# Six PSUM banks divided anew between two kinds of attention scores: from three and three to four and two

## The reference

```
x = x + attention(layernorm(x))          # 32 heads of 16, 8 key/value heads, so groups of 4 query heads
x = x + ffn(layernorm(x))                # silu(x Wg') * (x Wu') Wd', inner width 1376
attention: q, k rotated by position (rotary); att = q k' / 4, causal mask, softmax, times v, times Wo
```

## Time and profile before

| | us |
|---|---|
| median of 3 runs | 824.01 |
| lowest, highest | 822.51, 1285.82 |
| profiled execution, its own time | 827.75 |
| span of its profile, first to last instruction | 826.0 |
| granted TensorE clock, mean of the span | 0.978 |

### The profile page before, as it was taken

One profiled execution on the slowest core, in us unless ns is written; L12 is line 12 of the kernel. 1 busy time (PEld: TensorE's weight loads), 2 busy tenths in 40 slices (PEclk: granted clock), 3 DMA queues, 4 the chain that ended last, 5 costly groups with the idle time before them and its releaser, 6 DMA issues.

```text
span 826.0 us, 12351 instructions
## 1 busy us (share of the span) xinstructions
PE 778.1 (94%) x4449; PEld 529.0 (64%) x4480; DVE 437.5 (53%) x744; ACT 345.0 (42%) x684; POOL 208.0 (25%) x380
## 2 busy tenths in 40 slices
PE   3879999999999999999797999999999999999998
PEld 2645555555555554444385887888878888788886
DVE  6786878677876777887243543423314233241112
ACT  3326667766776677656542332211112111121111
POOL 3134774467526763233300000000000000000000
PEclk9959999999999999999998999999999999999999
DMA  7235677233232335471195110422003210020001
GB/s 254 72 102 175 218 247 230 80 97 111 74 112 73 108 97 185 130 206 36 41 291 151 51 39 13 141 64 66 25 14 130 73 55 34 13 102 0 1 1 51
DMA packets 74614, 81.86 MB, mean 99 GB/s; under 512 B 8721, under 2 KB 58385, under 8 KB 74353
## 3 DMA queue, kind: packets, MB, share of 16 engines
q1 hardware_dynamic: 74560, 81.16, 31.7%
HBM read 57.02 MB, written 33.36 MB: 109 GB/s over the span
## 4 chain that ended last, share of the span: by engine, by line
PE 46%; SPq 2%; DMA 1%; DVE 1%; issue 0%; ACT 0%; DVEq 0%
PE bank L1458 31%; PE ps_y L1510 14%; SPq L1277 1%; SPq L1274 1%; PE bank L1497 1%; DMA inverse<-scratch_inverse 0%; DMA wd_lo<-scratch_wd_raw 0%; DVE x_in L1440 0%; SPq L172 0%; SPq L173 0%; DVE x_res L1444 0%; DVE o_in L185 0%; DVE ctx_lo L195 0%; DVE wd_lo L1384 0%; ACT wd_hi L1332 0%
## 5 line engine op out<-in xcount | busy, mean ns | idle before, releaser
L846 DVE TENSOR_REDUCE m_raw<-ps_s 128x1 f32<-128x512 f32 (+3 forms) x352 | 210.8, 634 | 63.1 <-PE ps_s L1091 60.9
L716 ACT ACTIVATE probs<-ps_t 128x512 f32<-128x512 f32 (+1 forms) x352 | 185.8, 564 | 101.8 <-PE ps_t L1118 100.5
L1415 DVE TENSOR_TENSOR h<-h,bank 128x512 f32<-128x512 f32 (+1 forms) x44 | 30.2, 687 | 221.2 <-PE bank L1458 220.3
L1088 PE MATMUL ps_s<-k_rows,q_rows 96*128 96x256 bf16 (+3 forms) x512 | 132.6, 312 | 6.8 <-DVE m_raw L846 6.1
L1118 PE MATMUL ps_t<-q_rows,k_rows 98*128 98x512 bf16 (+1 forms) x352 | 126.3, 363 | 3.1 <-ACT probs L716 0.9
L1353 ACT ACTIVATE h<-bank 128x512 f32<-128x512 f32 (+1 forms) x44 | 26.3, 599 | 153.4 <-PE bank L1458 153.4
L1088 PEld LDWEIGHTS ps_s<-k_rows,q_rows 96*128 96x128 bf16 x512 | 44.4, 100 | 70.4 <-DVE m_raw L846 32.4
L1131 PE MATMUL ps_o<-probs,v_ones 128*32 128x512 f32 (+3 forms) x1024 | 84.3, 447 | 0.6 <-ACT o_sb L726 0.4
L624 POOL TENSOR_SCALAR_AFFINE_SELECT probs<-probs 128x512 f32<-128x512 f32 x128 | 84.6, 661 | 0.0
L1359 ACT CAST h_hi<-h 128x512 fp32r<-128x512 f32 (+1 forms) x44 | 27.4, 622 | 126.9 <-DVE h L1415 126.9
L217 POOL TENSOR_TENSOR var_eps<-mean_var,eps 128x1 f32<-128x1 f32 x16 | 3.0, 189 | 294.1 <-DVE mean_var L212 294.1
(11 more groups left out here) (146 smaller groups left out, 1349.3 us busy)
## 6 DMA issues: line engine op xcount, KB each, us to landing
scratch_o<-o_sb SPq DMA_DIRECT2D x31, 256.0 KB, 2.4
q_rows<-scratch_q_parts SPq DMA_DIRECT2D x32, 192.0 KB
x_in<-in_x SPq DMA_DIRECT2D x16, 256.0 KB, 4.9
scratch_q_parts<-r_top SPq DMA_DIRECT2D x32, 128.0 KB, 2.4
q_rows<-scratch_q_parts SPq DMA_DIRECT2D x32, 128.0 KB
x_res<-in_x SPq DMA_DIRECT2D x16, 256.0 KB, 2.8
o_in<-scratch_o SPq DMA_DIRECT2D x64, 64.0 KB
inverse<-scratch_inverse SPq DMA_DIRECT2D x64, 64.0 KB
```

Source lines behind the costliest of these rows:

```text
L716: nc.scalar.activation(probs[:, g % 2, heads * u:heads * (u + 1), CHUNK_AT[c]:CHUNK_AT[c + 1]], ps_t[:, pos % S_BANKS, 0:heads * CHUNK_N[c ...
L846: nc.vector.tensor_reduce(out=m_raw[:, g % 2, at:at + heads], op=ALU.max, axis=AXIS.X, in_=ps_s[:, (BANK_AT[i] + u) % S_BANKS, 0:heads * w ...
L1088: nc.tensor.matmul(bank[:, place], q_rows[r][0:ROWS, j, P * q:P * (q + 1)], k_rows[r][0:ROWS, 0:width], start=(place == 0), stop=False)
L1415: nc.vector.tensor_tensor(h[0:m, r], h[0:m, r], bank[units["up", f] % BANKS][0:m, :], ALU.mult).then_inc(h_ready, 1)
```

## The change

The six banks of `ps_s` and `ps_t` are divided four and two. `S_BANKS` becomes 4 and sets the banks of `ps_s` alone; a new constant `T_BANKS = 2` sets those of `ps_t`, in the position arithmetic, in `t_before`, and in `PRE_BANKS`, which falls from 4 to 3. No instruction is added or removed on any engine; only banks and the numbers that the waits wait for change.

```
-S_BANKS = 3
+S_BANKS, T_BANKS = 4, 2
...
-PRE_BANKS = 1 + S_BANKS
+PRE_BANKS = 1 + T_BANKS
...
 def t_before(n, pos):
-    return t_count(n, pos - S_BANKS) if pos >= S_BANKS else t_count(n - 1, pos + T_BANKS_OF - S_BANKS) if n else 0
+    return t_count(n, pos - T_BANKS) if pos >= T_BANKS else t_count(n - 1, pos + T_BANKS_OF - T_BANKS) if n else 0
...
-        ps_t = psum("ps_t", [P, S_BANKS, T])
+        ps_t = psum("ps_t", [P, T_BANKS, T])
...
-    nc.scalar.copy(m_t[n % 2][:], ps_t[rows, MAX_POS % S_BANKS, 0:P]).then_inc(exp_done, 1)
+    nc.scalar.copy(m_t[n % 2][:], ps_t[rows, MAX_POS % T_BANKS, 0:P]).then_inc(exp_done, 1)
...
-    ps_t[:, pos % S_BANKS, 0:heads * CHUNK_N[c]].rearrange("p (j t) -> p j t", j=heads),
+    ps_t[:, pos % T_BANKS, 0:heads * CHUNK_N[c]].rearrange("p (j t) -> p j t", j=heads),
...
-    to, ready = ps_t[:, MAX_POS % S_BANKS], scores_t_ready
+    to, ready = ps_t[:, MAX_POS % T_BANKS], scores_t_ready
...
-    nc.tensor.matmul(ps_t[:, pos % S_BANKS, 0:heads * width],
+    nc.tensor.matmul(ps_t[:, pos % T_BANKS, 0:heads * width],
```

## The result

The changed kernel takes 833.03 us (median of 4 runs, 832.57 to 836.99), the kernel before in the same session 823.26 (4 runs). The ratio is 1.0116, with an interval of 1.0088 to 1.0143: about 9.6 us slower, where 8.4 was forecast. One of the four runs of the kernel before took 1285.82 us; the ratio is of the undisturbed runs.

What follows compares the result with a forecast made beforehand. PE's own matmul stream was taken as the bound of the steady part. The terms 14.4 - 4.6 - 0.5 - 0.9 = +8.4 us gave 832.4 us for the median, with 824.5 to 840 for 8 in 10.

Steps and rivals of the forecast that it cites:

- PE's stream is the bound: Steady part: PE's own matmul stream sets the time, so every wait put into it moves the end.
- The rival in which the waits are swallowed: Regular groups: a chain through DVE or DMAs sets the period; only the `ps_s` gain remains, 819 us; chance 0.07.
- The 31 waits: Transposed maxima (L1102) wait for the exponential two positions before: 22 x 0.353, 6 x 0.488, 3 x 0.562, sum 12.4 us.
- Part 1: Cost of two banks for `ps_t`: 12.4 + 0.5 + 1.5 = 14.4 us, bounds 9.6 and 25.7.
- Part 2: Gain of four banks for `ps_s`, in ten single groups: 2.1 + 1.07 + 1.45 = 4.6 us, bounds nothing and 9.9.
- The nine groups that are not regular: Groups without projections or with extra ACT copies: PE's shift from position 4 covers nearly all late positions; cost 0.5 us.
- the cascade rival: Ring of two: a late matmul delays the matmul two on, every late position paid separately; +21 us, 845; chance 0.12.
- The last two groups: End of the loop: ACT sets the pace, 0.54 against 0.49 us a bank, plus one late position; cost 1.5 us.
- Part 3: Ahead of the first group: dense units over three banks cost 0; earlier transposed maxima bring 0.5 us back.
- The long wait: PE's 1.96 us wait at position 8 for a DVE reduce: 1.25 goes, about 0.7 stays near 372 us.
- part 4: Behind PE's longest wait, 373.5 to 377.7 us: clock at 0.59 costs 1.7 us; half, 0.9, was taken as gain.
- The clock: Rival: repeated PE stops bring the granted clock down, in every fourth group 14 us, 846 in all; chance 0.04.

Runs made afterwards that it cites:

- e2: The changed kernel with the transposed maxima issued behind the dense piece of the same place instead of ahead of it: 823.05 us, ratio 0.9993 to the kernel before.
- e6: The kernel before (three and three banks) with the transposed maxima issued behind the dense pieces: 822.51 us, ratio 0.9971.
- e1: The kernel before with two banks for `ps_t`, three for `ps_s` and the eighth bank unused: 834.75 us, ratio 1.0133.
- e3: The kernel before with only the dense units ahead of the first group rotating over three banks instead of four: 824.16 us, ratio 1.0005.
- e4: The kernel before, unchanged, run again for a second profile: 824.17 us, ratio 0.9994.
- e8: The kernel before (three and three banks) with the transposed maxima issued inside the next slot, between its two kinds of scores: 822.45 us, ratio 0.9974.
- e5: The changed kernel with the transposed maxima issued inside the next slot, between its two kinds of scores: 824.31 us, ratio 0.9999 to the kernel before.

## Why the prediction was right, and where its steps were not

**PE's stream is the bound, and a wait in it moves the end: right.** The regular period went from 11.13 to 11.47, forecast 11.48, and e2, which keeps the division and takes the wait away, brings the time from 833.03 to 823.05 us, the ratio from 1.0116 to 0.9993. That is 10.1 us, of which 2.4 come by the new place alone (e6); about 7.7 are left for the waits, where e2's text expected 8.7. The rival in which the waits are swallowed is out for the regular groups. (Its bar of "fewer than 5 of the 31 waits" has no working: by the prediction's own terms, 0.40 us a wait against gains of 5.1, the two are even at 13.)

**The 31 waits: right in place, and in size for 25 of them.** All 31 start 0.144 or 0.145 us behind the exponential two positions before. The 22 lose 0.35 us each (0.353 forecast), groups 6, 14 and 22 lose 0.56 (0.562), but groups 7, 15, 23, 24, 25 and 30 only 0.27 (0.488), since PE comes to them late from stops ahead. The sum is 11.0 where 12.4 was forecast. (The working speaks of one such wait and "six more" in the trace of before; there are six in all.)

**Part 1 as a sum: too large.** 14.4 us was forecast for two banks alone, e1 measures 10.9. The working priced the 31 waits and left the rest of the stream standing. But a PE that stops for 0.27 to 0.56 us at the transposed maxima reaches the next bank of `ps_s` that much later, and waits less for its maximum or not at all.

**Part 2: too large as well, with the other sign.** The 4.6 us of waits for maxima were counted as freed by the fourth bank. Most go with three banks as well, by part 1. Parts 1 and 2 each counted these microseconds once, as a cost that was not paid and as a gain that was already there. The cost was 3.5 us too high and the gains of the fourth bank 4.7 too high; the errors cancel in the total, which is luck, and the forecast of +8.4 against +9.6 does not show them. (Its sum of 2.1 for the small waits leaves out the 0.37 of the earlier trace rows; with it they are 2.5, and the forecast would have been 832.0. And the 0.27, in group 4, was no wait for a maximum but for a load, which a bank can't shorten; in the changed kernel 0.18 us of it is still there. The row of before:)

```profile
118.48 0.39 PE L1088 MATMUL ps_s<-k_rows,q_rows 96*128 96x512 bf16 x1 [0.22 <-DMA k_rows<-scratch_k_parts]
```

**The nine groups that are not regular.** "In the nine the shift that PE has already had from position 4 covers all but about 0.25 us in two of them" failed. In groups 22 to 25, taken together, the parts came to about +0.1 us (0.56 + 3 x 0.49 for the maxima, less about 1.9 that part 2 gave back); measured are 38.67 against 36.75, +1.9 (some of group 24's period is scatter, 9.07 us in before and 8.49 to 8.64 in e3, e4, e6 and e8, which would make it +2.3 to +2.5). These groups have no dense work (group 22 four small matmuls of it), so PE comes round to `ps_t` sooner than ACT has emptied it, several times in a group: T is 1.70, 0.80, 1.32 and 1.56 us. PE and ACT of the changed kernel in group 22:

```profile
311.63 0.22 PE L1102 MATMUL ps_t<-ident_b,m_parts 128*32 128x128 bf16 x1 [0.49 <-ACT probs L716]
...
316.93 0.39 PE L1118 MATMUL ps_t<-q_rows,k_rows 98*128 98x512 bf16 x1 [1.14 <-ACT probs L716]
...
314.85 1.04 ACT L677 COPY r_top<-rot 128x1024 bf16<-128x1024 bf16 x1
315.78 0.59 ACT L726 COPY o_sb<-ps_o 128x512 f32<-128x512 f32 x1
316.26 1.69 ACT L716 ACTIVATE probs<-ps_t 128x512 f32<-128x512 f32 x3
```

The later of the two waits follows two copies of ACT, 1.04 and 0.59 us long, ahead of the exponential that frees the bank; a third bank had covered them. The trace of before already held this lateness: there the same matmul of group 22 started 0.99 us ahead of the end of the exponential two positions before.

```profile
310.99 0.38 PE L1118 MATMUL ps_t<-q_rows,k_rows 98*128 98x512 bf16 x1
...
311.37 0.61 ACT L716 ACTIVATE probs<-ps_t 128x512 f32<-128x512 f32 x1
```

This is the cascade rival, true in groups 22 to 25, partly in 7 and 15 (+0.90 each, of which 0.39 is left in e2), and in no regular group; e5 shows that no place of the transposed maxima heals it.

**The last two groups:** forecast +1.5, measured 11.67 - 11.05 and 11.39 - 11.42, +0.6. With the clock moving group 30 between 10.04 and 11.67 us at the same two banks, this measures the waits badly.

**Part 3.** The rotation costs nothing, as said (e3). The gain ahead of the first group was 0.90 us for 0.5, and it is the one gain that belongs to the fourth bank beyond doubt: 15.50 to 15.51 us in before, e1, e3, e4, e6 and e8, 14.58 to 14.60 in the changed kernel, e2 and e5.

**The long wait and part 4.** I expected 0.7 us of it to stay near 372 and half of the clock's 1.7 to come back. PE lost 0.07 us there in the changed kernel, but 0.66 in e2 and 1.03 in e5, so 0.7 was a fair size. The clock stayed at 1.00 in all three. With three banks it fell in three profiles of five, and a fall goes with 1.7 to 2.3 us more in the group, which bears out the 1.7 and makes the half of it a fair guess. That the fourth bank prevents the fall is not shown: e1 and two others with three banks had none, and three profiles are few. At full clock group 28 takes 12.46 to 12.94 us with three banks and 11.53 to 12.14 with four, and group 29 takes most of the difference back.

**The clock.** It is 1.00 over 100 to 370 us with a stop of 0.35 us in each regular group and up to 1.14 in single ones. The Trainium skill, "TensorE: Matmul & The Clock Gate", section on psum-queue depth-cycling, tells of a kernel that cycles through PSUM banks and whose small idles between groups of matmuls made the clock swing; at the spacing of these stops, one in 11.47 us, this trace does not show it. The rule in "Perfetto Trace Analysis", section on optimization strategy, that a repeated gap on the engine that should be saturated can mean too few buffers, the trace bears out: the gap came with the third bank's going. The cure in e2 was another order, not another bank.

## What to carry to other kernels

When banks are moved from one ring to another, don't add the waits that one ring gains to those that the other loses: an engine that works through both in one order can stand only once, and the earlier stop covers the later. Price each ring by itself against an otherwise unchanged kernel (e1), since a right total can be the sum of two errors. And before giving a ring a bank, look at which position in it is late: here it was one of twelve, and putting one dense piece ahead of it won 10 us, about what the third bank was worth (10.9). Where a group has no such filler, the ring's length does count, and there the pace of the engine that empties it is the price.

## What the runs showed of the hardware that I had not expected

The place of a small matmul changes its cost without any wait. Between L1118 and the dense L1040, the transposed maxima (128x128, a 32-row result) make the group 0.07 to 0.12 us longer than behind the dense piece, as e6 shows against before (11.01 to 11.05 against 11.12 to 11.14). In e2's rows 0.33 us pass from the dense matmul to L1102 and 0.16 on to L1088, 0.49 where L1040 to L1088 alone is 0.23, so 0.26 is added; in the old place 0.31 to it, 0.14 on to L1040 and 0.34 to the next L1040 make 0.79, where 0.46 is usual (0.03 and 0.43), so 0.33 is added. What in PE makes the difference no run took apart. After a release, too, L1102 is the slower starter: 0.144 us behind the end of an exponential, 0.055 for L1118.

The clock is the other thing. A stop of PE of 1.75 us in e4 was followed by a granted clock of 0.51 over 372.5 to 376.0 us, and one of 1.76 us in e6 was not (see e4).
